# Scores and messages of an attention layer on a graph, made four tiles at a time: where the loop over the engines closes

## The chip, the cores and the metric

One Trainium2 chip, one core of it. The time is the device time of one execution in microseconds (us), median of three runs. The engines are TensorE (PE, with PEld for its weight loads), VectorE (DVE), ScalarE (ACT), GpSimd (POOL, which here issues the indirect transfers) and SyncE (SP, which issues the plain ones). Each has its own queue of instructions and takes them in order; engines wait for each other by semaphores that only count up.

## The reference

Two layers of attention on a graph of 6250 nodes and 100000 edges, sorted by target node, 8 heads of 16 features, 8 relations:

```python
k, q, v = (typed_linear(x, ntype, W).reshape(n, H, HS) for W in (Wk, Wq, Wv))
...
kw = rel_apply(k[src], etype, Watt)
a = (kw * q[dst]).sum(-1) * pri[:, etype].T / SQRT_D
amax = jax.ops.segment_max(a, dst, num_segments=n)
ex = jnp.exp(a - amax[dst])
den = jax.ops.segment_sum(ex, dst, num_segments=n)
alpha = ex / (den[dst] + 1e-16)
m = rel_apply(v[src], etype, Wmsg)
agg = jax.ops.segment_sum(alpha[..., None] * m, dst, num_segments=n)
```

Behind it come a typed linear, a gate, a layer norm, and after the second layer an output product.

## The kernel before

A node stage puts key and value of each node and relation, already multiplied by the relation's matrices, into a table in memory (`node_kv`, 256 numbers a row), and the queries into `node_q`. The edge stage (`edge_stage`, L1141) then goes over the edges once for each of the two layers. Edges are cut into 784 tiles of 128 (one edge a partition), 14 tiles are a batch (`G`), and there are 56 batches. Within a batch tiles are taken in fours (`FOURS`: 4, 4, 4 and 2 tiles).

Three batches are in flight. Step b of the stage works on batch b ("new"), b - 1 ("mid") and b - 2 ("old"), and each engine has its part of the step written out by hand in a function `step`, whose order is the order of its queue.

- POOL gathers the rows of the edges' sources from `node_kv`, one transfer a tile (L1243), into `rows`, which has three buffers. The tiles of four of batch b + 1 may be gathered as soon as TensorE has summed the same four of batch b - 2.
- SP loads for every tile the window of 128 queries that its targets lie in (`qw`, L1216) and the ranks of the edges in it.
- New: VectorE makes a one-hot matrix of the ranks (`one_hot`, L1259); TensorE spreads the queries to the edges with it (`spread`, L1499), and VectorE multiplies keys by them in place (`products`, L1270). A reduction over 16 features gives the scores (`scores`, L1275), `score[P, 14, 8]`. TensorE also turns the one-hot matrix (`turn`, L1488), and ScalarE copies it (L1424).
- Mid: TensorE transposes the scores of the batch (L1511), 8 x 14 rows. VectorE finds maxima over the runs of equal targets by scans (`own_maxima`, L1286 to L1292), ScalarE takes the exponential (L1439), VectorE sums and divides (`own_shares`, L1297 to L1305). TensorE transposes the result back (`alpha_ps`, L1526). `joined_tops` (L1310 to L1318) and `joined_sums` (L1323 to L1338) carry runs over tile borders; the latter's last instruction writes `share`. TensorE multiplies it out (`scale_ps`, L1539), ScalarE copies it (L1457). `messages` (L1355) multiplies the values by alpha in place.
- Old: TensorE sums the messages to target nodes (`sums`, L1480), VectorE multiplies the first column by the scale (`gains`, L1348), ScalarE adds all of it to `acc` (`means`, L1415 and L1419).

At the end of its step ScalarE makes the flags for the next maxima (`flags`, L1431 and L1432), and `own_maxima` waits for them and for the transposed scores. TensorE's step begins with two spreads of new and the transpose of mid's scores, and ends with the product for the scale.

Of the kernel before, what the change touches and what calls it, by code (L numbers as in the profile page):

```python
# [25 lines left out]
P = 128  # L26
N = 6250
E = 100000
D = 128
H = 8  # L30
HS = D // H
# [10 lines left out]
U = 3  # L42
# [1090 lines left out]
SIZES = (G,) * (B - 1) + (14,)  # L1133
BATCHES = len(SIZES)
FIRST = tuple(sum(SIZES[:b]) for b in range(BATCHES + 1))
FOURS = tuple(tuple(range(g, min(g + FOUR, n)) for g in range(0, n, FOUR)) for n in SIZES)
GROUP = tuple(sum(len(fours) for fours in FOURS[:b]) for b in range(BATCHES + 1))
# [3 lines left out]
def edge_stage(nc, c, s, rows_in, spent, l, tab, scratch, acc, weights):  # L1141
# [10 lines left out]
    with ExitStack() as st:  # L1152
# [8 lines left out]
        score = sb("score", [P, G, H])  # L1161
# [39 lines left out]
        with nc.Block(no_gpsimd_drain=True) as block:  # L1201
# [48 lines left out]
            def _(dve):  # L1250
# [18 lines left out]
                    dve.wait_ge(s["spread"], GROUP[b] + k + 1)  # L1269
                    v.tensor_tensor(half, half, ps_q[(GROUP[b] + k) % 2][:, 0:len(four), :], ALU.mult).then_inc(s["prod"], 1)  # L1270

                def scores(b):
                    n = SIZES[b]
                    dve.wait_ge(s["prod"], GROUP[b + 1])
                    v.reduce_sum(score[:, 0:n, :], rows[b % U][:, 0:n, 0:D].rearrange("p g (h d) -> p g h d", h=H),  # L1275
                                 axis=AX.X).then_inc(s["score"], 1)

                def of_tiles(a, rows_):
# [3 lines left out]
                def own_maxima(b):  # L1282
                    m = SIZES[b] * H
                    dve.wait_ge(s["score_t"], b + 1)
                    dve.wait_ge(s["flags"], 2 * b + 2)
                    v.tensor_tensor_scan(fwd[0:m, :], seam[0:m, 0:P], score_t[0:m, :], -BIG, ALU.add, ALU.max).then_inc(s["chain"], 1)  # L1286
                    dve.wait_ge(s["chain"], b * CHAIN + 1)
                    v.tensor_tensor_scan(top[0:m, ::-1], seam[0:m, 1:P + 1][:, ::-1], fwd[0:m, ::-1], -BIG, ALU.add, ALU.max).then_inc(s["chain"], 1)
                    dve.wait_ge(s["chain"], b * CHAIN + 2)
                    v.tensor_tensor(shifted[0:m, :], score_t[0:m, :], top[0:m, :], ALU.subtract).then_inc(s["shifted"], 1)  # L1290
                    mask, two = of_tiles(top, m)
                    v.tensor_tensor(ends[0:m, 0:2, :], mask, two, ALU.mult).then_inc(s["ends"], 1)  # L1292
# [55 lines left out]
                    v.tensor_tensor(gained[q % 2][:, 0:len(four)], ps_sum[q % 2][:, 0:len(four), 0], scale[b % 2][:, 1, four[0]:four[-1] + 1],  # L1348
                                    ALU.mult).then_inc(s["gained"], 1)

                def messages(b):
                    n = SIZES[b]
                    dve.wait_ge(s["alpha_ps"], b + 1)
                    half = rows[b % U][:, 0:n, D:2 * D].rearrange("p g (h d) -> p g h d", h=H)
                    v.tensor_tensor(half, half, alpha_ps[:, 0:n * H].rearrange("p (g h o) -> p g h o", h=H, o=1).to_broadcast([P, n, H, HS]),  # L1355
                                    ALU.mult).then_inc(s["message"], 1)

                def step(b):
                    new, mid, old = in_flight(b)
                    has = lambda batch, k: batch is not None and k < len(FOURS[batch])  # L1360
                    if has(new, 0):
                        products(new, 0)
                    if mid is not None:
                        own_maxima(mid)
                    if has(old, 0):
                        gains(old, 0)
                    if has(new, 1):
                        products(new, 1)
                    if b + 1 < BATCHES:
                        one_hot(b + 1)  # L1370
                    if mid is not None:
                        own_shares(mid)
                    if has(old, 1):
                        gains(old, 1)
                    if has(new, 2):
                        products(new, 2)
                    if mid is not None:
                        joined_tops(mid)
                    if has(new, 3):
                        products(new, 3)  # L1380
                    if has(old, 2):
                        gains(old, 2)
                    if mid is not None:
                        messages(mid)
                        joined_sums(mid)
                    if has(old, 3):
                        gains(old, 3)
                    if new is not None:
                        scores(new)

                v.memset(acc[:, :], 0.0).then_inc(s["zeroed"], 1)
                v.memset(tops[:, 0:1], -BIG).then_inc(s["zeroed"], 1)
# [76 lines left out]
            def _(pe):  # L1469
                t = nc.tensor  # L1470

                def sums(b, k):
                    q = GROUP[b] + k
                    if k == 0:
                        pe.wait_ge(s["message"], b + 1)
                        pe.wait_ge(s["turned"], GROUP[b + 1])
                    if q >= 2:
                        pe.wait_ge(s["joined"], UNTIL[q - 2])
                    for n, g in enumerate(FOURS[b][k]):
                        ins = t.matmul(ps_sum[q % 2][:, n, :], rows[b % U][:, g, D:2 * D], hot[b % U][:, g, :], start=True, stop=True)  # L1480
                    ins.then_inc(s["sums"], 1)
# [20 lines left out]
                def step(b):  # L1502
# [4 lines left out]
                            spread(new, k)  # L1507
                    if mid is not None:
                        m = SIZES[mid] * H
                        pe.wait_ge(s["score"], mid + 1)  # L1510
                        t.transpose(score_t[0:m, :], score[:, 0:SIZES[mid], :].rearrange("p g h -> p (g h)"), c["ident"][:, :]).then_inc(s["score_t"], 1)  # L1511
                    if has(old, 0):
                        sums(old, 0)
# [97 lines left out]
```

## Time and profile before

| what | value |
|---|---|
| median of three runs | 2824.23 us (2822.65 to 2825.16) |
| the profiled execution | 2824.39 us, of which the span from first to last instruction is 2822.7 us |
| PE busy | 1902.4 us (67%) |
| VectorE busy | 2146.3 us (76%) |
| ScalarE busy | 1519.7 us (54%) |
| POOL busy | 1971.6 us (70%) |
| granted TensorE clock, mean | 0.772 |

A row of the timeline gives the start, the duration, the engine, the line, the operation, what it writes and reads, and in brackets how long the engine stood idle before it and what it waited for. Busy shares are means over node stages and edge stages; neither edge stage's limit can be read from them.

### The profile page before, as it was taken

How to read it: one execution, taken by the hardware profiler on the slowest of the kernel's cores; microseconds unless marked ns; L12 is line 12 of the kernel's file. 1: busy time of each engine (PE TensorE's matmuls, PEld its weight loads, DVE VectorE, ACT ScalarE, POOL GpSimd, SP SyncE). 2: the span in 40 equal slices, each digit the busy share in tenths (PEclk: the TensorE clock that was granted, in tenths of full speed). 3: DMA queues.
4: the chain of work that ended last, by engine and by line, in shares of the span. 5: the costliest groups of instructions: out<-in, count | busy, mean ns of one | idle time of the engine just before them, and what ended most of it. 6: DMA issues, size and time to landing. Idle time of an engine off the chain costs nothing. (4 is left out here: it accounts for less than half of the span.)

```text
span 2822.7 us, 53679 instructions
## 1 busy us (share of the span) xinstructions
PE 1902.4 (67%) x12612; PEld 1692.1 (60%) x12612; DVE 2146.3 (76%) x5513; ACT 1519.7 (54%) x5159; POOL 1971.6 (70%) x2072
## 2 busy tenths in 40 slices
PE   1877747766777767776577747777777767667466
PEld 1755536666666666666455546666666666666344
DVE  6977758777777777777577757777777777777587
ACT  0027625555555555555577725555555555555555
POOL 3716667777777777777277777777777777777176
PEclk8569968777787787777688967778778787787655
DMA  5528876666666666665266776666666666665411
GB/s 135 88 109 346 342 204 186 185 184 183 186 184 184 185 184 185 185 185 169 68 244 276 292 203 184 184 184 183 184 185 183 183 184 184 183 184 163 116 45 37
DMA packets 396315, 512.23 MB, mean 181 GB/s; under 512 B 75449, under 2 KB 311419, under 8 KB 383508
## 3 DMA queue, kind: packets, MB, share of 16 engines
q0 software_dynamic: 102144, 327.28, 37.3%
q1 hardware_dynamic: 284760, 179.79, 21.8%
q10 hardware_dynamic: 9104, 1.86, 0.4%
q8 instruction: 97, 1.59, 0.2%
q14 instruction: 210, 1.72, 0.2%
HBM read 383.54 MB, written 142.96 MB: 187 GB/s over the span
## 5 line engine op out<-in xcount | busy, mean ns | idle before, releaser
L1243 POOL DMA_INDIRECT g_rows<-node_kv,g_ids x1568 | 1485.0, 947 | 474.8 <-issue 444.2
L1499 PE MATMUL g_ps_q<-g_qw,g_hot_t 128*128 128x128 f32 x3136 | 593.7, 357 | 61.8 <-DMA g_qw<-node_q 50.0
L1419 ACT ACTIVATE acc<-acc,g_gained,g_scale x1568 | 600.9, 383 | 3.0 <-issue 2.1
L1499 PEld LDWEIGHTS g_ps_q<-g_qw,g_hot_t 128*128 128x128 f32 x3136 | 546.6, 265 | 71.2 <-DMA g_qw<-node_q 51.6
L1415 ACT ACTIVATE acc<-g_ps_sum 128x127 f32 x1568 | 411.5, 262 | 317.5 <-DVE g_gained L1348 257.3
L1480 PE MATMUL g_ps_sum<-g_hot,g_rows 128*128 128x128 f32 x3136 | 553.6, 331 | 5.9 <-ACT acc L1419 5.7
L1480 PEld LDWEIGHTS g_ps_sum<-g_hot,g_rows 128*128 128x128 f32 x3136 | 512.0, 245 | 12.5 <-ACT acc L1419 8.4
L1270 DVE TENSOR_TENSOR g_rows<-g_rows,g_ps_q 128x512 f32<-128x512 f32 x448 | 274.5, 613 | 317.4 <-DMA g_rows<-node_kv,g_ids 290.0
L1488 PE MATMUL g_ps_hot<-ident,g_hot_t 128*128 128x128 f32 x1568 | 293.3, 312 | 18.2 <-ACT g_hot L1424 17.9
L1424 ACT ACTIVATE g_hot<-g_ps_hot 128x512 f32<-128x512 f32 x448 | 233.2, 521 | 56.1 <-PE g_ps_hot L1488 56.1
L1488 PEld LDWEIGHTS g_ps_hot<-ident,g_hot_t 128*128 128x128 f32 x1568 | 230.2, 169 | 28.0 <-ACT g_hot L1424 25.1
L1539 PE MATMUL g_ps_b<-g_share,head_of_feature 8*128 8x28 f32 x224 | 61.5, 359 | 264.2 <-DVE g_share L1338 259.3
L1525 PE MATMUL g_ps_a<-g_ends,head_of_row 112*8 112x56 f32 x224 | 30.6, 221 | 292.4 <-DVE g_alpha L1305 292.4
L1259 DVE TENSOR_TENSOR g_hot_t<-g_rank_row,g_ps_a 128x1792 f32<-128x1792 bf16 x112 | 225.5, 2014 | 0.1
L1539 PEld LDWEIGHTS g_ps_b<-g_share,head_of_feature 8*128 8x128 f32 x224 | 47.9, 264 | 295.6 <-DVE g_share L1338 290.2
L1275 DVE TENSOR_REDUCE g_score<-g_rows 128x112 f32<-128x1792 f32 x112 | 225.0, 2009 | 0.1
L1355 DVE TENSOR_TENSOR g_rows<-g_rows,g_ps_b 128x1792 f32<-128x1792 f32 x112 | 224.5, 2005 | 0.0
L1089 POOL DMA_INDIRECT n_ag<-node_agg,node_slot x112 | 116.9, 1044 | 137.5 <-DMA node_agg<-n_agg 46.4
L1439 ACT ACTIVATE g_exp_t<-g_shifted 112x128 f32<-112x128 f32 x112 | 34.7, 310 | 312.9 <-DVE g_shifted L1290 312.9
L1525 PEld LDWEIGHTS g_ps_a<-g_ends,head_of_row 112*8 112x8 f32 x224 | 13.5, 87 | 316.0 <-issue 316.0
L1052 PE MATMUL n_wide<-bd,n_kv_t 32*128 32x256 f32 x1792 | 140.9, 431 | 79.5 <-DVE n_kv L865 39.9
L865 DVE COPY n_kv<-n_wide 128x512 f32<-128x512 f32 x224 | 143.9, 684 | 49.3 <-PE n_wide L1052 36.3
(243 smaller groups left out, 3265.1 us busy)
## 6 DMA issues: line engine op xcount, KB each, us to landing
g_qw<-node_q SPq DMA_DIRECT2D x1568, 64.0 KB
g_rank_row<-edge_rank SPq DMA_DIRECT2D x112, 448.0 KB
g_rows<-node_kv,g_ids POOLq DMA_INDIRECT x1568
node_agg<-n_agg SPq DMA_DIRECT2D x24, 256.0 KB, 3.1
node_rows<-node_x SPq DMA_DIRECT2D x2, 1792.0 KB
node_q<-l_blank_q SPq DMA_DIRECT2D x1, 3200.0 KB
node_q<-n_q_sb,node_slot POOLq DMA_INDIRECT x112
node_kv<-n_kv,node_id POOLq DMA_INDIRECT x112
```

The lines of the kernel that those rows point to most:

```text
L865: v.tensor_copy(kv[i % KV][:, :, :, q * 32:(q + 1) * 32].rearrange("p r a f -> p a r f"), wide[:, q, :].rearrange("p (a r f) -> p a r f", ...
L1243: g_.indirect_dma_start(out=rows[b % U][:, g, :], out_offset=None, in_=scratch["kv"][:, :], in_offset=bass.IndirectOffsetOnAxis(ap=ids[b / ...
L1259: v.tensor_tensor(hot_t[b % 2][:, 0:n, :].rearrange("p g e -> p (g e)"), rank_row[:, 0:n * P], number_ps.to_broadcast([P, n * P]), ALU.is_ ...
L1270: v.tensor_tensor(half, half, ps_q[(GROUP[b] + k) % 2][:, 0:len(four), :], ALU.mult).then_inc(s["prod"], 1)
L1275: v.reduce_sum(score[:, 0:n, :], rows[b % U][:, 0:n, 0:D].rearrange("p g (h d) -> p g h d", h=H), axis=AX.X).then_inc(s["score"], 1)
L1355: v.tensor_tensor(half, half, alpha_ps[:, 0:n * H].rearrange("p (g h o) -> p g h o", h=H, o=1).to_broadcast([P, n, H, HS]), ALU.mult).then ...
L1415: a.activation(acc[:, bass.ds(w + 1, P - 1)], ps_sum[q % 2][:, n, 1:P], ACT.Copy).then_inc(s["copied"], 1)
L1419: a.activation(at, at, ACT.Identity, scale=scale[b % 2][:, 0, g:g + 1], bias=gained[q % 2][:, n:n + 1]).then_inc(s["joined"], 1)
L1424: a.activation(hot[b % U][:, four[0]:four[-1] + 1, :], ps_hot[q % 2][:, 0:len(four), :], ACT.Copy).then_inc(s["turned"], 1)
L1480: ins = t.matmul(ps_sum[q % 2][:, n, :], rows[b % U][:, g, D:2 * D], hot[b % U][:, g, :], start=True, stop=True)
L1488: ins = t.transpose(ps_hot[q % 2][:, n, :], hot_t[b % 2][:, g, :], c["ident"][:, :])
L1499: ins = t.matmul(ps_q[q % 2][:, n, :], hot_t[b % 2][:, g, :], qw[b % 2][:, g, :], start=True, stop=True)
```

## The change

VectorE's `scores` and `messages` get a second argument, the number of the four tiles, and do only these; `step` calls them piece by piece. The scores of the new batch stood at the end of the step; their pieces now stand behind `own_maxima`, behind `own_shares`, behind the third products and behind the third gains. The four pieces of the messages stand where the one instruction stood, behind the last of the scores. TensorE's waits for scores, messages and turned one-hot matrices count fours of tiles.

```diff
-                def scores(b):
-                    n = SIZES[b]
-                    dve.wait_ge(s["prod"], GROUP[b + 1])
-                    v.reduce_sum(score[:, 0:n, :], rows[b % U][:, 0:n, 0:D].rearrange("p g (h d) -> p g h d", h=H),
+                def scores(b, k):
+                    part_ = slice(FOURS[b][k][0], FOURS[b][k][-1] + 1)
+                    dve.wait_ge(s["prod"], GROUP[b] + k + 1)
+                    v.reduce_sum(score[:, part_, :], rows[b % U][:, part_, 0:D].rearrange("p g (h d) -> p g h d", h=H),
                                  axis=AX.X).then_inc(s["score"], 1)
...
-                def messages(b):
-                    n = SIZES[b]
-                    dve.wait_ge(s["alpha_ps"], b + 1)
-                    half = rows[b % U][:, 0:n, D:2 * D].rearrange("p g (h d) -> p g h d", h=H)
-                    v.tensor_tensor(half, half, alpha_ps[:, 0:n * H].rearrange("p (g h o) -> p g h o", h=H, o=1).to_broadcast([P, n, H, HS]),
+                def messages(b, k):
+                    first, n = FOURS[b][k][0], len(FOURS[b][k])
+                    if k == 0:
+                        dve.wait_ge(s["alpha_ps"], b + 1)
+                    half = rows[b % U][:, first:first + n, D:2 * D].rearrange("p g (h d) -> p g h d", h=H)
+                    v.tensor_tensor(half, half, alpha_ps[:, first * H:(first + n) * H].rearrange("p (g h o) -> p g h o", h=H, o=1).to_broadcast([P, n, H, HS]),
                                     ALU.mult).then_inc(s["message"], 1)
...
                     if mid is not None:
                         own_maxima(mid)
+                    if has(new, 0):
+                        scores(new, 0)
...
                     if mid is not None:
                         own_shares(mid)
+                    if has(new, 1):
+                        scores(new, 1)
...
                     if has(new, 2):
                         products(new, 2)
+                        scores(new, 2)
...
+                    if has(new, 3):
+                        scores(new, 3)
+                    for k in range(4):
+                        if has(mid, k):
+                            messages(mid, k)
                     if mid is not None:
-                        messages(mid)
                         joined_sums(mid)
                     if has(old, 3):
                         gains(old, 3)
-                    if new is not None:
-                        scores(new)
...
-                    if k == 0:
-                        pe.wait_ge(s["message"], b + 1)
-                        pe.wait_ge(s["turned"], GROUP[b + 1])
+                    pe.wait_ge(s["message"], q + 1)
+                    pe.wait_ge(s["turned"], q + 1)
...
-                        pe.wait_ge(s["score"], mid + 1)
+                        pe.wait_ge(s["score"], GROUP[mid + 1])
```

VectorE's queue from the last instruction of `joined_sums` to the first gains of the next step, before (`g_score` are the scores, `g_top` the maxima, `g_share` the share, `g_gained` the gains):

```order
L1338 TENSOR_TENSOR g_share<-g_part,g_whole 8x28
L1348 TENSOR_TENSOR g_gained<-g_ps_sum,g_scale 128x2
L1275 TENSOR_REDUCE g_score<-g_rows 128x112
L1270 TENSOR_TENSOR g_rows<-g_rows,g_ps_q 128x4x128
L1286 SCALAR_TENSOR_TENSOR g_ps_a<-g_seam,g_ps_a 112x128
L1288 SCALAR_TENSOR_TENSOR g_top<-g_seam,g_ps_a 112x128
L1290 TENSOR_TENSOR g_shifted<-g_ps_a,g_top 112x128
L1292 TENSOR_TENSOR g_ends<-tile_mask,g_top 112x28
L1348 TENSOR_TENSOR g_gained<-g_ps_sum,g_scale 128x4
```

The same place in the changed kernel:

```order
L1338 TENSOR_TENSOR g_share<-g_part,g_whole 8x28
L1348 TENSOR_TENSOR g_gained<-g_ps_sum,g_scale 128x2
L1270 TENSOR_TENSOR g_rows<-g_rows,g_ps_q 128x4x128
L1286 SCALAR_TENSOR_TENSOR g_ps_a<-g_seam,g_ps_a 112x128
L1288 SCALAR_TENSOR_TENSOR g_top<-g_seam,g_ps_a 112x128
L1290 TENSOR_TENSOR g_shifted<-g_ps_a,g_top 112x128
L1292 TENSOR_TENSOR g_ends<-tile_mask,g_top 112x28
L1275 TENSOR_REDUCE g_score<-g_rows 128x32
L1348 TENSOR_TENSOR g_gained<-g_ps_sum,g_scale 128x4
```

The reduction has gone from between the share and the next batch's first products, and a piece of it stands behind the maxima. The other pieces of the same step and those of the messages, further down the queue of the changed kernel (`g_alpha` is alpha; rows of small instructions between are left out by the dots):

```order
L1305 TENSOR_TENSOR g_alpha<-g_exp_t,g_ps_a 112x128
L1275 TENSOR_REDUCE g_score<-g_rows 128x32
L1348 TENSOR_TENSOR g_gained<-g_ps_sum,g_scale 128x4
L1270 TENSOR_TENSOR g_rows<-g_rows,g_ps_q 128x4x128
L1275 TENSOR_REDUCE g_score<-g_rows 128x32
...
L1270 TENSOR_TENSOR g_rows<-g_rows,g_ps_q 128x2x128
L1348 TENSOR_TENSOR g_gained<-g_ps_sum,g_scale 128x4
L1275 TENSOR_REDUCE g_score<-g_rows 128x16
L1356 TENSOR_TENSOR g_rows<-g_rows,g_ps_b 128x4x128 x3
L1356 TENSOR_TENSOR g_rows<-g_rows,g_ps_b 128x2x128
L1323 SCALAR_TENSOR_TENSOR g_coeff<-tile_pass_sb,g_grown 8x14
```

All of these pieces now stand between `own_maxima` and the share. TensorE's queue from the product for the scale on has the same instructions in the same order in both; of before, with the semaphores that each waits for:

```order
L1539 MATMUL g_ps_b<-g_share,head_of_feature 128x28 [waits edges_share]
L1499 MATMUL g_ps_q<-g_qw,g_hot_t 128x128 [waits edges_prod,edges_hot_t,edges_q_in1]
L1499 MATMUL g_ps_q<-g_qw,g_hot_t 128x128 x3
L1499 MATMUL g_ps_q<-g_qw,g_hot_t 128x128 [waits edges_prod]
L1499 MATMUL g_ps_q<-g_qw,g_hot_t 128x128 x3
L1511 MATMUL g_ps_a<-ident,g_score 112x128 [waits edges_score]
```

The transpose of the scores stays the last of these.

## Rows read from the trace of the kernel before

**Rows 1.** Waits of POOL, whole span, and a group of the page.
```profile
POOL g_rows L1243 <- PE g_ps_sum L1480: 23.8, 78, 0.3
...
L1243 POOL DMA_INDIRECT g_rows<-node_kv,g_ids x1568 | 1485.0, 947 | 474.8 <-issue 444.2
```

**Rows 2.** Timeline of VectorE, `own_maxima` of steps 1, 2 and 55, both layers.
```profile
397.12 0.42 DVE L1286 TENSOR_TENSOR_SCAN g_ps_a<-g_seam,g_ps_a 112x128 f32<-112x128 bf16 x1
...
413.25 0.43 DVE L1286 TENSOR_TENSOR_SCAN g_ps_a<-g_seam,g_ps_a 112x128 f32<-112x128 bf16 x1 [0.78 <-PE g_ps_a L1511]
...
1342.98 0.43 DVE L1286 TENSOR_TENSOR_SCAN g_ps_a<-g_seam,g_ps_a 112x128 f32<-112x128 bf16 x1 [0.87 <-PE g_ps_a L1511]
...
1658.46 0.42 DVE L1286 TENSOR_TENSOR_SCAN g_ps_a<-g_seam,g_ps_a 112x128 f32<-112x128 bf16 x1
...
1674.85 0.42 DVE L1286 TENSOR_TENSOR_SCAN g_ps_a<-g_seam,g_ps_a 112x128 f32<-112x128 bf16 x1
...
2605.44 0.43 DVE L1286 TENSOR_TENSOR_SCAN g_ps_a<-g_seam,g_ps_a 112x128 f32<-112x128 bf16 x1 [0.53 <-PE g_ps_a L1511]
```

**Rows 3.** Timeline of VectorE, one step of layer 1, to the next maxima.
```profile
1902.93 0.42 DVE L1286 TENSOR_TENSOR_SCAN g_ps_a<-g_seam,g_ps_a 112x128 f32<-112x128 bf16 x1
...
1904.57 0.16 DVE L1348 TENSOR_TENSOR g_gained<-g_ps_sum,g_scale 128x4 f32<-128x4 f32 x1 [0.34 <-issue]
...
1911.03 0.69 DVE L1270 TENSOR_TENSOR g_rows<-g_rows,g_ps_q 128x512 f32<-128x512 f32 x1 [1.49 <-DMA g_rows<-node_kv,g_ids]
1911.63 0.22 DVE L1310 TENSOR_TENSOR_SCAN g_tops<-tile_pass_sb,g_tops,g_ps_a 8x14 f32<-8x14 bf16 x1
...
1912.45 0.40 DVE L1270 TENSOR_TENSOR g_rows<-g_rows,g_ps_q 128x256 f32<-128x256 f32 x1
1912.78 0.14 DVE L1348 TENSOR_TENSOR g_gained<-g_ps_sum,g_scale 128x4 f32<-128x4 f32 x1
1912.85 2.00 DVE L1355 TENSOR_TENSOR g_rows<-g_rows,g_ps_b 128x1792 f32<-128x1792 f32 x1
1914.78 0.15 DVE L1323 SCALAR_TENSOR_TENSOR g_coeff<-tile_pass_sb,g_grown 8x14 f32<-8x14 bf16 x1
...
1916.16 0.18 DVE L1338 TENSOR_TENSOR g_share<-g_part,g_whole 8x28 f32<-8x28 f32 x1
...
1916.35 2.01 DVE L1275 TENSOR_REDUCE g_score<-g_rows 128x112 f32<-128x1792 f32 x1
...
1920.98 0.43 DVE L1286 TENSOR_TENSOR_SCAN g_ps_a<-g_seam,g_ps_a 112x128 f32<-112x128 bf16 x1 [0.39 <-PE g_ps_a L1511]
```

**Rows 4.** Timeline of TensorE, end of the same step and start of the next.
```profile
1913.31 0.44 PE L1488 MATMUL g_ps_hot<-ident,g_hot_t 128*128 128x128 f32 x2 [0.81 <-ACT g_hot L1424]
1916.40 0.62 PE L1539 MATMUL g_ps_b<-g_share,head_of_feature 8*128 8x28 f32 x2 [2.65 <-DVE g_share L1338]
1916.95 3.78 PE L1499 MATMUL g_ps_q<-g_qw,g_hot_t 128*128 128x128 f32 x16
1920.52 0.42 PE L1511 MATMUL g_ps_a<-ident,g_score 128*112 128x128 f32 x1
```

**Rows 5.** Windows: length, then busy time by engine, granted clock (PEclk), DMA share, GB/s.
```profile
1916.95:1920.94 3.99, 3.99 (x19) 3.99 (x19) 2.10 (x2) 2.01 (x8) 3.08 (x4) 0.50 0.75 213
...
619.20:621.80 2.60, 2.57 (x22) 2.53 (x23) 2.00 (x2) 1.76 (x8) 2.13 (x4) 1.00 0.78 200
```

**Rows 6.** Timeline of VectorE and TensorE, the same place of a step in layer 0.
```profile
619.00 0.18 DVE L1338 TENSOR_TENSOR g_share<-g_part,g_whole 8x28 f32<-8x28 f32 x1
...
619.23 0.40 PE L1539 MATMUL g_ps_b<-g_share,head_of_feature 8*128 8x28 f32 x2 [1.98 <-DVE g_share L1338]
...
621.45 0.27 PE L1511 MATMUL g_ps_a<-ident,g_score 128*112 128x128 f32 x1
```

**Rows 7.** Timeline: the flags in the step of rows 3; layer 0's tail.
```profile
1919.04 0.39 ACT L1432 ACTIVATE g_same<-seam_flags,ones 112x129 bf16<-112x129 bf16 x1
...
1358.88 0.43 DVE L1286 TENSOR_TENSOR_SCAN g_ps_a<-g_seam,g_ps_a 112x128 f32<-112x128 bf16 x1 [1.18 <-ACT g_same L1432]
```

## The prediction

> **What bounds the kernel now.** I read the waits of POOL first. Each of the 1568 gathers of edge rows keeps POOL busy 0.95 us, and the 444.2 us of idle time before them are its own issue, about 0.3 us each; the waits for TensorE's sums come to 23.8 us in 78 pieces of at most 0.3 us, which is that same issue time [rows 1]. So POOL never stands still for a buffer. In the edge stage a batch of 14 gathers sets the pace: `own_maxima` (L1286), whose start I call M, comes in step 2 of layer 0 at 413.25 and in step 55 at 1342.98, which is 17.54 us a step; in layer 1 it is (2605.44 - 1674.85) / 53 = 17.56 [rows 2]. I use 17.55.
>
> The next question is how near a second bound is. The steps are tied together by a **loop over three engines**, which I followed in the timeline of VectorE and of TensorE. From M, VectorE works down to `joined_sums`, whose last instruction (L1338) writes the share; call its end S. TensorE's queue then has the two scale matmuls (L1539), which wait for the share, the eight `spread` matmuls of the next batch (16 records), and only then the transpose of the scores (L1511), without which the next M cannot come.
>
> First half: M at 1902.93, S at 1916.16 + 0.18 = 1916.34, so 13.41 us [rows 3]. It holds two waits that are not work of the loop: 0.34 before the first gains and 1.49 before the third products, for a transfer. Without them, and with the 0.08 us of overlap that each of the two starts would have back, 13.41 - 0.34 - 1.49 - 0.16 = 11.42 us.
>
> Second half: the scale matmuls start 0.06 after S, the spreads at 1916.95, and the transpose ends at 1920.52 + 0.42 = 1920.94, 4.60 after S; M follows 0.04 later, and the row names this transpose as what it waited for [rows 3, 4]. It is that long since TensorE runs at 1.2 GHz (granted clock 0.50) [rows 5], after it stood idle 2.65 us for the share [rows 4]. The other form is at 2.4 GHz: after 1.98 us of idle time the transpose ends at 621.45 + 0.27 = 621.72, 2.54 after S at 619.18 [rows 5, 6]. I measured S to the end of the transpose in 106 steps: 83 lie between 4.0 and 4.6, mean 4.46, after idle times of 2.5 us in the mean; 16 lie under 3.5, nearly all after some 1.6 to 2 us.
>
> So the loop now needs 11.42 + 4.46 + 0.04 = 15.9 us of 17.55, and has **1.6 us to spare**. That is why POOL sets the pace. Note what stands in the second half on VectorE: the 2.01 us of `scores`, at 1916.35, just behind S. It fills time in which VectorE would wait for TensorE, and costs the loop nothing.
>
> **The change, part by part.**
> 1. Scores in four pieces, moved. One reduction of 1792 elements a row goes from behind S, and four come between M and S. A reduction and a multiply of 1792 elements take the same, 2.01 and 2.00, so I price pieces by the multiply: 512 elements last 0.69 and the next instruction starts 0.60 after it; 256 last 0.40, the next 0.33 after [rows 3]. Pieces 0 and 1 add 0.60 each. Piece 2 stands directly behind the products that it reads and waits for their end: 0.69 + 0.03 (a dependent pair has about 0.03 between) = 0.72. Piece 3, with a gain between, 0.35. Sum 2.27.
> 2. Messages in four pieces: 3 x 0.60 + 0.33 = 2.13, against 1914.78 - 1912.85 = 1.93 for one: 0.20.
> 3. First half of the loop: 11.42 + 2.27 + 0.20 = 13.89. Waits inside go: the third products now come to their turn 1.2 us later, so their transfer is mostly there.
> 4. Second half: the scores are ready long before, but TensorE takes the transpose in its turn, behind share, scale and spreads. Nothing of the 4.46 + 0.04 goes. The idle time before the scale matmuls grows: TensorE's last work before it ended at 1913.31 + 0.44 = 1913.75 [rows 4], 10.8 after M; 13.89 - 10.8 = 3.1 us idle instead of 2.65, so the slow form is the rule.
> 5. Loop: 13.89 + 4.50 = **18.39 us**, 0.84 over POOL's 17.55. The loop is now the pace. POOL's three batches of buffers don't help, since the loop is serial from the first batch to the last; POOL is only made to wait.
> 6. TensorE's finer waits (`message` and `turned` by four tiles): nothing. Behind them in its queue stand the turns and the next spreads, but both signals come a step earlier, so the sums still follow the transpose at once.
> 7. What the score pieces push back: the first gains by 0.6 us and the second by 1.2, and ScalarE's means with them. Covered: ScalarE's next meeting with the loop is the scale, behind S, and S itself is 2.5 later. The one-hot comes 0.6 later in its step and is used in the next. No DMA is added or moved on any queue.
>
> The skill has another figure for item 1. The Trainium skill, "VectorE: DVE Perf Modes", in the section on the TRN2 errata, gives a fixed 58 cycles (60 ns) for an instruction on SBUF data in its table, and says below it that 150 are measured. The trace sides with the second: (2.00 - 0.69) us over 1280 elements leaves 0.69 - 0.52 = 0.17 us fixed [rows 3]. By 60 ns the six extra instructions would cost 0.36 us of busy time and the loop would be some 0.3 us shorter, which would be an estimate of 2890 us.
>
> **Sum**, against the profiled execution's own time, 2824.4 us (span 2822.7 and 1.7 around it; the median of the three runs is 2824.23, so both agree to 0.01%):
> - 2 layers x 53 steps x 0.84 = 89;
> - the head: M of step 1 is bound by the first transfers and stays, at 397.12 and 1658.46. A step without gains is 0.2 shorter: 18.2 later are 415.3 and 1676.7, against 413.25 and 1674.85 [rows 2]: 2.1 + 1.8 = 4;
> - the tail of a layer: M to S is 12.7 in step 55 (1358.88 less 3.2 for the flags, as in A, less 1342.98 [rows 2, 7]) and grows to 13.9; step 56 has the 0.2 of the messages: 1.4 a layer, 3 in all. Behind S here ScalarE's flags decide (the wait of 1.18 at 1358.88 [rows 7]), as before.
>
> Together 96, so 2824.4 + 96 = **2921 us**, 3.4% slower.
>
> **Bounds of what the trace does not show.** Low: pieces with no fixed cost (1.93 + 0.13 for scores, nothing for messages) make the first half 13.48; with 4.13 + 0.04, the lower of the two lengths that the slow form mostly has, the loop is 17.65, and 106 x 0.10 + 5 gives 2840. High: 0.05 more for each of the eight pieces and always 4.64 make 14.29 + 4.64 = 18.93; 106 x 1.38 + 8 gives 2979. I take the middle since the 512-element row is the very shape.
>
> **Rivals.**
> A. *TensorE at full clock, and the loop stays hidden* (not slower). If the transpose ends 2.54 after S, ScalarE's path decides: the scale, two tiles' means and the flags end at 1919.04 + 0.39 = 1919.43, 3.09 after S [rows 7], and M 0.1 later. The loop is 13.89 + 3.19 = 17.08, under 17.55; only the tails stay: 2824.4 + 3 = 2827. The point of decision is 3.66 from S to M. For it: 16 steps of 106. Against: they came after short idle times, and the change lengthens them. Page's rule that would give this: the Trainium skill, "TensorE: Matmul & The Clock Gate", in Part 1, says that for modelling the cold ramp is under 1% of a typical kernel's span. By that rule the half clock would be left out and the time would be A's; here the trace disagrees, with 4.60 against 2.54 us in a loop that is run 112 times. Chance 0.11.
> B. *TensorE stays slow for more of the step.* Now it returns to full clock about 5 us after the scale matmuls. If the low clock held on until alpha is transposed, joined tops would wait and the loop would gain some 0.5 us: 18.9, 106 x 0.5 = 53 more, 2974. For it: less of each step busy. Against: the order of TensorE's work up to that point is unchanged. Chance 0.09.
> C. *Faster*: scores that are ready earlier save TensorE some waiting for them in the tail. But behind that the wait for the flags stands [rows 7], and POOL's gathers, 1.25 us each, are untouched; at most 3 us in all. With all that I may have overlooked, 0.03.
> The forecast has 0.76, and what is left, 0.01, is no change by other ways.
>
> **How the numbers follow.** What a measurement can tell from no change is 0.2%, 5.6 us. Slower: forecast and B, 0.85. Same: A and the rest, 0.12. Faster: 0.03. The range takes in most of the span between the bounds and B: 2850 to 2985; outside lie A, C and the outermost costs, about 0.2.
>
> **What would show it.** In the new profile: starts of `own_maxima` 18.4 us apart; POOL's gathers waiting for sums, some 90 us in all and up to a us or more at a time; VectorE's waits for gathered rows, like the 1.49 us of [rows 3], mostly gone, and in their place a wait of over a us before each `own_maxima` for the transpose; the idle time before the scale matmuls about 3.1 us, and TensorE at 0.50 behind it. It is wrong if the starts stay 17.55 apart: then the step to look at is S to M (item 4), or the price of the pieces (item 1).

## The result, and the profile after

| | before | after |
|---|---|---|
| median | 2824.69 us (4 runs, 2822.65 to 2826.42) | 2901.11 us (4 runs, 2897.57 to 2912.1) |
| span of the profiled execution | 2822.7 us | 2898.8 us |
| VectorE busy | 2146.3 us | 2193.7 us |
| POOL busy | 1971.6 us | 1972.3 us |
| granted TensorE clock, mean | 0.772 | 0.758 |

The changed kernel takes 1.0277 times as long, 95% interval 1.0249 to 1.0306: slower by 2.8%. The forecast was 2921 us, 3.4% slower.

First the pace. Timeline of VectorE in the changed kernel, `own_maxima` of steps 2 and 55 of both layers, which answers to [rows 2]:

```profile
410.83 0.43 DVE L1286 TENSOR_TENSOR_SCAN g_ps_a<-g_seam,g_ps_a 112x128 f32<-112x128 bf16 x1 [0.89 <-PE g_ps_a L1518]
...
1380.73 0.43 DVE L1286 TENSOR_TENSOR_SCAN g_ps_a<-g_seam,g_ps_a 112x128 f32<-112x128 bf16 x1 [0.64 <-ACT g_same L1440]
...
1713.62 0.43 DVE L1286 TENSOR_TENSOR_SCAN g_ps_a<-g_seam,g_ps_a 112x128 f32<-112x128 bf16 x1 [0.22 <-PE g_ps_a L1518]
...
2682.00 0.43 DVE L1286 TENSOR_TENSOR_SCAN g_ps_a<-g_seam,g_ps_a 112x128 f32<-112x128 bf16 x1 [1.16 <-PE g_ps_a L1518]
```

(1380.73 - 410.83) / 53 = 18.30 us a step in layer 0 and 18.27 in layer 1, against 17.54 and 17.56. POOL no longer sets it. Its waits over the whole span, which answer to [rows 1], each row with us in total, times and longest:

```profile
POOL g_rows L1243 <- issue: 438.6, 1427, 2.1
POOL g_rows L1243 <- PE g_ps_sum L1487: 100.8, 108, 2.5
```

The waits for TensorE's sums were 23.8 us in pieces of at most 0.3; now they are 100.8 us, up to 2.5 us at once. The gathers are as cheap as before, but are held up. On VectorE the transfer has almost gone out of the waits. Whole span, before and then after:

```profile
DVE g_rows L1270 <- DMA g_rows<-node_kv,g_ids: 290.0, 181, 6.8
```

```profile
DVE g_rows L1270 <- PE g_ps_q L1506: 275.3, 111, 14.8
DVE g_ps_a L1286 <- PE g_ps_a L1518: 110.7, 102, 1.2
...
DVE g_rows L1270 <- DMA g_rows<-node_kv,g_ids: 14.8, 3, 7.5
```

What VectorE waits for at a step's start is now TensorE, once for the spread queries and once more for the transposed scores, in nearly each of the 112 steps. One such start in the timeline of the changed kernel, with the slow form of TensorE's stretch (answers to [rows 4]):

```profile
1927.38 0.18 DVE L1338 TENSOR_TENSOR g_share<-g_part,g_whole 8x28 f32<-8x28 f32 x1
...
1927.61 0.62 PE L1546 MATMUL g_ps_b<-g_share,head_of_feature 8*128 8x28 f32 x2 [3.22 <-DVE g_share L1338]
1928.16 3.78 PE L1506 MATMUL g_ps_q<-g_qw,g_hot_t 128*128 128x128 f32 x16
...
1930.34 0.69 DVE L1270 TENSOR_TENSOR g_rows<-g_rows,g_ps_q 128x512 f32<-128x512 f32 x1 [2.70 <-PE g_ps_q L1506]
1931.73 0.42 PE L1518 MATMUL g_ps_a<-ident,g_score 128*112 128x128 f32 x1
...
1932.19 0.43 DVE L1286 TENSOR_TENSOR_SCAN g_ps_a<-g_seam,g_ps_a 112x128 f32<-112x128 bf16 x1 [1.16 <-PE g_ps_a L1518]
```

S, the end of the share, is 1927.56; from there to M at 1932.19 are 4.63 us, as before. Of these VectorE waits 2.70 and 1.16. Before, the reduction of the scores lay in that time.

### The profile page after: what moved, and what is told of

Its sections match the earlier page's. It is cut to its first block and busy times, and to the rows that moved or that the text cites. A ratio compares the mean times of both kernels' runs of the same rounds, so it can differ in the third digit from the quotient of the medians.

```text
span 2898.8 us, 54687 instructions
## 1 busy us (share of the span) xinstructions
PE 1923.1 (66%) x12612; PEld 1721.1 (59%) x12612; DVE 2193.7 (76%) x6185; ACT 1523.5 (53%) x5159; POOL 1972.3 (68%) x2072
## 5 line engine op out<-in xcount | busy, mean ns | idle before, releaser
L1506 PE MATMUL g_ps_q<-g_qw,g_hot_t 128*128 128x128 f32 x3136 | 601.9, 360 | 56.6 <-DMA g_qw<-node_q 49.3
L1506 PEld LDWEIGHTS g_ps_q<-g_qw,g_hot_t 128*128 128x128 f32 x3136 | 553.5, 267 | 63.9 <-DMA g_qw<-node_q 50.8
L1487 PE MATMUL g_ps_sum<-g_hot,g_rows 128*128 128x128 f32 x3136 | 574.7, 340 | 11.8 <-ACT acc L1427 11.8
L1487 PEld LDWEIGHTS g_ps_sum<-g_hot,g_rows 128*128 128x128 f32 x3136 | 539.4, 256 | 19.3 <-issue 18.8
L1270 DVE TENSOR_TENSOR g_rows<-g_rows,g_ps_q 128x512 f32<-128x512 f32 x448 | 273.2, 610 | 290.2 <-PE g_ps_q L1506 275.3
L1275 DVE TENSOR_REDUCE g_score<-g_rows 128x32 f32<-128x512 f32 x448 | 274.8, 613 | 4.1
L1356 DVE TENSOR_TENSOR g_rows<-g_rows,g_ps_b 128x512 f32<-128x512 f32 x448 | 246.5, 611 | 0.0
```

Of the source, the lines that this page charges most:

```text
L1275: v.reduce_sum(score[:, part_, :], rows[b % U][:, part_, 0:D].rearrange("p g (h d) -> p g h d", h=H), axis=AX.X).then_inc(s["score"], 1)
L1356: v.tensor_tensor(half, half, alpha_ps[:, first * H:(first + n) * H].rearrange("p (g h o) -> p g h o", h=H, o=1).to_broadcast([P, n, H, HS ...
L1506: ins = t.matmul(ps_q[q % 2][:, n, :], hot_t[b % 2][:, g, :], qw[b % 2][:, g, :], start=True, stop=True)
```

## The experiments

The loop theory: M to S on VectorE, and S to the next M through TensorE, add up to a step as soon as they are over POOL's 17.55 us. It has two rivals: the six extra instructions cost their time wherever they stand, or VectorE is simply too full. In the table below, M to S and S to M are means over steps 4 to 55 of both layers of the profiled execution; a step is the mean from step 2 to 55.

| kernel | M to S | S to M | step, layers 0 and 1 | median | ratio to before, 95% interval |
|---|---|---|---|---|---|
| before | 13.02 | 4.51 | 17.54, 17.56 | 2824.7 | 1 |
| changed | 14.04 | 4.20 | 18.30, 18.27 | 2901.1 | 1.0277 (1.0249 to 1.0306) |
| all score pieces behind the share | 13.17 | 4.42 | 17.61, 17.58 | 2827.3 | 0.9997 (0.9988 to 1.0007) |
| scale behind the transpose | 14.34 | 3.20 | 17.56, 17.56 | 2830.9 | 1.0013 (1.0004 to 1.0023) |
| TensorE kept busy | 14.38 | 3.22 | 17.58, 17.60 | 2829.8 | 1.0005 (0.9995 to 1.0015) |
| 0.6 us more in the loop | 14.71 | 4.08 | 18.89, 18.79 | 2962.5 | 1.0470 (1.0452 to 1.0487) |

The four lower kernels ran in one session, beside runs of the kernel before with a median of 2828.25 us. Where POOL sets the pace, the halves hold waits for transfers and add up to its pace.

**1. The same pieces, back at the old place.** If the number of instructions is what costs, this stays slow.

```diff
-                    if has(new, 0):
-                        scores(new, 0)
...
-                    if has(new, 1):
-                        scores(new, 1)
...
-                        scores(new, 2)
...
-                    if has(new, 3):
-                        scores(new, 3)
...
                     if has(old, 3):
                         gains(old, 3)
+                    if has(new, 0):
+                        scores(new, 0)
+                    if has(new, 1):
+                        scores(new, 1)
+                    if has(new, 2):
+                        scores(new, 2)
+                    if has(new, 3):
+                        scores(new, 3)
```

> The changed kernel with all four score pieces put back behind the share (end of VectorE's step); scores and messages stay in four pieces, TensorE's finer waits stay. Loop theory: M to S falls from 14.0 to 11.8 us, the pieces lie in the time in which VectorE waits for the transpose, the loop needs some 16 us and POOL's 17.55 us a step is the pace again: 2824 to 2828 us. Rival (the six extra instructions a step cost it, wherever they stand: 112 steps x 0.46 to 0.92 us of VectorE time): 2875 to 2895 us.

Measured 2827.33 us, 0.9997 of before. This kernel has all the cuts of the change, four score pieces and four message pieces, and TensorE's finer waits. The cutting alone costs nothing that can be told, as long as the score pieces lie behind the share. VectorE's waits for transfers are back, 156 of them where the kernel before had 181:

```profile
DVE g_rows L1270 <- DMA g_rows<-node_kv,g_ids: 224.3, 156, 6.7
```

**2. The other half shortened: TensorE's order.** VectorE's queue stays as changed. The scale's product leaves the head of the line.

```diff
                         pe.wait_ge(s["score"], GROUP[mid + 1])
+                        if old is not None:
+                            pe.wait_ge(s["chain"], old * CHAIN + 12)
                         t.transpose(score_t[0:m, :], score[:, 0:SIZES[mid], :].rearrange("p g h -> p (g h)"), c["ident"][:, :]).then_inc(s["score_t"], 1)
+                    if old is not None:
+                        pe.wait_ge(s["share"], old + 1)
+                        t.matmul(scale_ps[:, 0:2 * SIZES[old]], c["head_of_feature"][:, :], share[:, :, 0:SIZES[old]], start=True, stop=True).then_inc(s["scale_ps"], 1)
...
-                    if mid is not None:
-                        pe.wait_ge(s["share"], mid + 1)
-                        t.matmul(scale_ps[:, 0:2 * SIZES[mid]], c["head_of_feature"][:, :], share[:, :, 0:SIZES[mid]], start=True, stop=True).then_inc(s["scale_ps"], 1)
```

> The changed kernel, VectorE untouched; on TensorE the scale matmuls move from the end of a step to behind the transpose of the scores in the next step, and the transpose waits for the last read of the shared PSUM bank by joined_sums, some 1.1 us before S, in place of the share. Loop theory: spreads and transpose run before S, the second half becomes ScalarE's path, 3.1 to 3.2 us; loop 14.0 + 3.15 = 17.2 us, under POOL's 17.55: 2824 to 2832 us. Rival (VectorE is simply too full, 14 us and more in a row): no or little change, 2890 to 2905 us.

Measured 2830.93 us, 1.0013 of before: of the 76 us, 2.7 are left against the kernel before of the same session, with no instruction of VectorE moved or taken away. So VectorE is not too full. A step's start in its timeline (`own_maxima` is L1286, the scale L1523 here):

```profile
1017.70 0.16 DVE L1327 TENSOR_TENSOR g_add<-g_add,g_ps_a 8x14 f32<-8x14 f32 x1
1018.00 0.29 PE L1520 MATMUL g_ps_a<-ident,g_score 128*112 128x128 f32 x1 [0.38 <-DVE g_add L1327]
1018.84 0.18 DVE L1338 TENSOR_TENSOR g_share<-g_part,g_whole 8x28 f32<-8x28 f32 x1
...
1019.07 0.40 PE L1523 MATMUL g_ps_b<-g_share,head_of_feature 8*128 8x28 f32 x2 [0.78 <-DVE g_share L1338]
```

In this step the transpose ends 0.7 us before S (0.4 in the mean); in the changed kernel it ends 4.1 us behind S in the mean. S to M is now 3.2 us, which is the way through ScalarE's flags. The transpose goes no earlier in this kernel, since it writes into the tile `ps_a`, from which VectorE still reads the ends of the sums, and I made TensorE wait for the last of these reads.

**3. TensorE's clock.** The same order as in the changed kernel, but eight matmuls without use fill the idle time before the scale; they write where the next spread writes.

```diff
+                    if mid is not None and new is not None:
+                        if b + 1 < BATCHES:
+                            pe.wait_ge(s["prod"], GROUP[b + 1] - 1)
+                        for _ in range(8 if b + 1 < BATCHES else 0):
+                            t.matmul(ps_q[GROUP[b + 1] % 2][:, 0, :], c["ident"][:, :], c["ident"][:, :], start=True, stop=True)
```

> The changed kernel plus eight matmuls without use on TensorE (identity by identity into the bank that the next spread overwrites) in its idle time before the scale matmuls. If the half clock behind the idle time makes the second half long: share to transpose falls from 4.14 us (mean) to about 2.55, ScalarE's 3.15 us decide, loop 17.2 us, 2824 to 2835 us. If the clock has nothing to do with it: no gain, or slower by up to 1 us a step where the extra matmuls hold up the share's product, 2900 to 3000 us.

Measured 2829.82 us, 1.0005 of before. S to the end of the transpose is 2.56 us in the mean (2.54 to 3.50), from 4.14. The rows of one step:

```profile
1000.62 1.95 PE L1548 MATMUL g_ps_q<-ident 128*128 128x128 f32 x16
1002.74 0.17 DVE L1338 TENSOR_TENSOR g_share<-g_part,g_whole 8x28 f32<-8x28 f32 x1
...
1002.97 0.40 PE L1551 MATMUL g_ps_b<-g_share,head_of_feature 8*128 8x28 f32 x2 [0.40 <-DVE g_share L1338]
1003.30 2.05 PE L1506 MATMUL g_ps_q<-g_qw,g_hot_t 128*128 128x128 f32 x16
...
1005.18 0.27 PE L1518 MATMUL g_ps_a<-ident,g_score 128*112 128x128 f32 x1
```

The 16 spread records take 2.05 us here and 3.78 in the row at 1928.16 above. More work on TensorE made the kernel 71 us faster than the changed one, since TensorE comes out of the wait at 2.4 GHz: S to the end of the transpose is nowhere over 3.50 us now, where it was in 97 of 108 steps of the changed kernel (mean granted clock 0.813, from 0.758).

**4. The dose.** One reduction without use, 512 elements a row, in the loop; its result goes to a tile that nobody reads.

```diff
                     if has(new, 0):
                         scores(new, 0)
+                        v.reduce_sum(idle_[:, :], c["ones"][:, :].rearrange("p (o e) -> p o e", o=1).to_broadcast([P, FOUR, P]), axis=AX.X)
```

> The changed kernel plus one reduction without use (512 elements a row, about 0.61 us start to start) on VectorE behind the first score piece, between M and S. Loop theory: every step is 0.61 us longer, 106 x 0.61 = 65 and 1 for the tails: 2965 us. If VectorE had slack between M and S: about 2901 us.

Measured 2962.54 us, 1.0470 of before; the span is 2962.6 - 2898.8 = 63.8 us over the changed kernel's, where 65 for the steps and 1 for the tails were expected. A step grew by 0.59 us in layer 0 and 0.52 in layer 1, and POOL's waits for the sums with it:

```profile
POOL g_rows L1244 <- PE g_ps_sum L1489: 167.1, 136, 2.8
```

**5. Four kernels in sessions that answer less.** These ran twice, on two different chips, and there the kernel before itself took 3470.4 and 3459.4 us instead of 2828 (and 6360.3 us in one of its 13 runs in the first session).

The extra reduction behind the share (the end of VectorE's step) instead of in the loop:

```diff
                     if has(old, 3):
                         gains(old, 3)
+                    if new is not None:
+                        v.reduce_sum(idle_[:, :], c["ones"][:, :].rearrange("p (o e) -> p o e", o=1).to_broadcast([P, FOUR, P]), axis=AX.X)
```

> The changed kernel plus the same reduction without use (about 0.61 us), but behind the share, at the end of VectorE's step. Loop theory: it lies in the wait for the transpose and costs nothing: 2898 to 2905 us. If VectorE's busy time as such is the bound: 2965 us.

> The changed kernel plus the reduction without use (0.61 us) behind the share, run again since the kernel before took 3470 us in the session of the first try. Loop theory: it lies in the wait for the transpose and costs nothing: 2898 to 2905 us. If VectorE's busy time as such is the bound: 2965 us, as with the same instruction between M and S.

The messages in one instruction (`messages` is that of the kernel before again), the scores as changed:

```diff
-                    for k in range(4):
-                        if has(mid, k):
-                            messages(mid, k)
                     if mid is not None:
+                        messages(mid)
                         joined_sums(mid)
...
-                    pe.wait_ge(s["message"], q + 1)
+                    pe.wait_ge(s["message"], b + 1)
```

> The changed kernel with the messages in one instruction again, scores still in pieces between M and S. Loop theory: M to S is 0.20 us shorter, 107 x 0.20 = 21 less: 2880 us. Rival (pieces of the messages let TensorE start its sums earlier): 2901 us or slower.

> The changed kernel with the messages in one instruction, again for the same reason. Loop theory: M to S 0.20 us shorter, 21 us less: 2880 us. Rival (pieces of the messages let TensorE start its sums earlier): 2901 us or slower.

The kernel before with its one score instruction ahead of the messages:

```diff
+                    if new is not None:
+                        scores(new)
                     if mid is not None:
                         messages(mid)
...
-                    if new is not None:
-                        scores(new)
```

> The kernel before with its one score instruction moved ahead of the messages; nothing is cut in pieces. Loop theory: M to S is 11.42 + 1.98 = 13.4 us, the second half 4.2 (its mean in the changed kernel) to 4.5 us, loop 17.6 to 17.9 us: just over POOL's pace, 2830 to 2862 us. Rival (the cutting alone does the harm): 2824 us.

> The kernel before with its one score instruction moved ahead of the messages, again for the same reason. Loop theory: M to S 13.4 us, loop 17.6 to 17.9 us, 2830 to 2862 us. Rival (the cutting alone does the harm): 2824 us.

The last two score pieces behind the share, the first two as changed:

```diff
                         products(new, 2)
-                        scores(new, 2)
...
-                    if has(new, 3):
-                        scores(new, 3)
...
                         gains(old, 3)
+                    if has(new, 2):
+                        scores(new, 2)
+                    if has(new, 3):
+                        scores(new, 3)
```

> The changed kernel with the last two score pieces (768 of 1792 elements) behind the share and the first two where the change put them. Loop theory: M to S 14.04 - 1.07 = 12.97 us, loop 17.2 to 17.5 us, just under POOL's pace: 2825 to 2832 us. Rival (harm in proportion to the pieces that are moved): about 2860 us.

> The changed kernel with the last two score pieces behind the share, again for the same reason. Loop theory: M to S 12.97 us, loop 17.2 to 17.5 us, just under POOL's pace: 2825 to 2832 us. Rival (harm in proportion to what is moved): about 2860 us.

| kernel | first session | second session |
|---|---|---|
| before | 3470.4 | 3459.4 |
| half of the pieces behind the share | 3473.3, 0.9976 (0.9932 to 1.0020) | 3471.1, 1.0045 (1.0005 to 1.0084) |
| messages whole | 3513.6, 1.0119 (1.0051 to 1.0187) | 3509.3, 1.0143 (1.0067 to 1.0218) |
| changed, extra reduction behind the share | 3529.2, 1.0182 (1.0127 to 1.0237) | 3531.3, 1.0214 (1.0139 to 1.0290) |
| whole scores moved | 3669.4, 1.0591 (1.0533 to 1.0649) | 3662.0, 1.0570 (1.0483 to 1.0657) |

No expected time can be held against these. Where the time goes can be seen in part. In the traces of these kernels some instructions begin late although their engine is idle and the work they wait for has ended. One such place in the kernel with the reduction behind the share (second session), and then the same place in the changed kernel (`products` is L1271 and L1270; "remote" is a releaser that the profile can't name):

```profile
1017.78 1.09 PE L1509 MATMUL g_ps_q<-g_qw,g_hot_t 128*128 128x128 f32 x4
...
1019.74 0.15 DVE L1319 TENSOR_TENSOR g_below<-g_before,g_joint 8x14 f32<-8x14 f32 x1
1022.07 0.42 DVE L1271 TENSOR_TENSOR g_rows<-g_rows,g_ps_q 128x256 f32<-128x256 f32 x1 [2.17 <-remote]
```

```profile
1957.77 1.09 PE L1506 MATMUL g_ps_q<-g_qw,g_hot_t 128*128 128x128 f32 x4
...
1959.74 0.15 DVE L1318 TENSOR_TENSOR g_below<-g_before,g_joint 8x14 f32<-8x14 f32 x1
1959.82 0.40 DVE L1270 TENSOR_TENSOR g_rows<-g_rows,g_ps_q 128x256 f32<-128x256 f32 x1
```

The fourth products wait, by the program, for the spreads alone, which ended at 1018.87. In this kernel they begin over 1 us late in 43 of 102 steps and `joined_tops`, which waits for TensorE's product of the ends, in 52; in the changed kernel neither does once. Together these two come to 2.7 us a step, nearly all of what M to S has grown by (17.0 us from 14.04). Why, the profile doesn't show: whether the signal or the instruction itself came late is open. With such late starts a step takes over 21 us even with half of the pieces behind the share.

Only what these kernels say of each other in one session is left, and that is little. Half of the pieces behind the share costs 0.5% at most in the mean, as the loop theory has it; harm in proportion, the 2860 us of the expectation, would be some 1.2%. Moving the one whole instruction ahead of the messages, with nothing cut, is the dearest, 5.7 to 5.9%, where no theory expected more than 1.3%. Its third gains begin over 1 us late in 70 of 102 steps (up to 4.9 us, second session), so that the scores and messages behind them, 4 us of work, all come late; with the fourth products that is 4.1 us a step. So its size can't be read as the price of the place, and the place without the cutting stays untested in an undisturbed session. That the cutting alone does no harm is shown by experiment 1. That the reduction behind the share is free, and that whole messages give 21 us back, stays open: the changed kernel had no run in these sessions. The two kernels differ by 16 and 22 us, which would fit both. If VectorE's busy time were the bound, they should differ by 64 us or more; how far that holds in a disturbed session isn't known.

## Why the prediction was right

**What bounds before, and the loop (right).** Every reading of [rows 1 to 6] that carried the sum held: POOL was the pace, the loop the second bound with room to spare, and the room was filled by the moved pieces. Experiments 2 and 3 shorten the second half of the loop in two different ways, by TensorE's order and by its clock (the mean granted clock of the kernel rises in both, to 0.803 and 0.813), and both return to 17.6 us a step; experiment 4 lengthens the first half and is paid nearly in full.

**Items 1 to 3, the first half (right, 0.15 short).** Forecast 13.89 us, measured 14.04, median 13.97. The pieces last what the multiply's row said: 613 ns in the mean for the score pieces and 611 for the message pieces, each over three of 512 elements and one of 256, against 613 ns for the products before. From the third products to S, 5.31 + 0.72 + 0.35 + 0.20 = 6.58 was forecast, and 6.58 is the least measured (5.31 was the least before); the mean is 6.78. What a cut costs there is not the fixed term of a duration: an independent instruction starts some 0.08 us before the end of the one before it, and by item 2 a cut costs 0.20 / 3 = 0.07 us.

The fixed term itself is best read from the score reductions, which read SBUF alone (products and messages read PSUM too): 2009 ns over 1792 elements before, 680 over 512 in the pieces (ahead of the second bar a row gives the busy time in us and the mean of one in ns):

```profile
L1275 DVE TENSOR_REDUCE g_score<-g_rows 128x112 f32<-128x1792 f32 x112 | 225.0, 2009 | 0.1
```

```profile
L1275 DVE TENSOR_REDUCE g_score<-g_rows 128x32 f32<-128x512 f32 x336 | 228.4, 680 | 3.9
```

At the pace of the 1280 elements between, 512 take 532 ns, and some 150 ns are left. That agrees with the 150 cycles (some 155 ns) that the Trainium skill, "VectorE: DVE Perf Modes", section on the TRN2 errata, calls measured, and not with the 58 (60 ns) of its table. The prediction's estimate of 2890 us by the table has a step that isn't worked out, "some 0.3 us shorter": items 1 and 2 price the six extra instructions at 2.27 + 0.20 - 1.93 = 0.54 us. At the 0.36 us that the prediction takes from the table a step would be 0.18 us shorter, which makes an estimate of 2902 us. That 2890 or 2902 lies nearer to the measured time than 2921 does is chance, since the pieces cost what the rows said and the difference lies in the second half, the head and the tail.

**Where the other 0.2 us of some steps come from (a part of rival B).** TensorE has a second idle time in a step, before alpha. In steps 4 to 54 of both layers, 102 in all, the eight records of the sums behind it (L1487) take 1.06 us, which is the full clock, in 13 steps, 1.91 or 1.92, the half clock, in 51, and something between in 38. Before it was 38, 35 and 29. M to S is 13.87 us in the mean in the 13 and 14.19 in the 51. The changed kernel, step 15 of layer 1:

```profile
1957.26 0.34 PE L1532 MATMUL g_ps_a<-g_ends,head_of_row 112*8 112x56 f32 x2 [3.38 <-DVE g_alpha L1305]
...
1958.65 1.91 PE L1487 MATMUL g_ps_sum<-g_hot,g_rows 128*128 128x128 f32 x8
...
1960.66 0.16 DVE L1348 TENSOR_TENSOR g_gained<-g_ps_sum,g_scale 128x4 f32<-128x4 f32 x1 [0.44 <-issue]
...
1964.58 0.18 DVE L1338 TENSOR_TENSOR g_share<-g_part,g_whole 8x28 f32<-8x28 f32 x1
...
1964.81 0.40 PE L1546 MATMUL g_ps_b<-g_share,head_of_feature 8*128 8x28 f32 x2 [2.11 <-DVE g_share L1338]
1965.14 2.05 PE L1506 MATMUL g_ps_q<-g_qw,g_hot_t 128*128 128x128 f32 x16
```

And the clock over the two stretches (the number before the DMA share):

```profile
1957.26:1959.20 1.94, 1.94 (x10) 1.76 (x11) 1.91 (x5) 1.30 (x6) 1.33 (x3) 0.50 0.60 211
1965.14:1967.30 2.16, 2.16 (x20) 2.16 (x20) 0.69 (x1) 1.69 (x8) 1.75 (x2) 1.00 0.77 214
```

After 3.38 us of idle time the sums run at half clock, the third gains come 0.44 late, and the share with them. But then the clock is full when the share comes, and the spreads take 2.05 us. What this step loses in its first half, it gains more than back in the second. So it goes in 11 of the 51 steps, the only ones of the 102 in which S to the end of the transpose stays under 3.5 us; in the other 40 the second half is of the slow form as well.

**Item 4, the second half (right that nothing of it goes, 0.3 too long).** Forecast 4.50, measured 4.20. I put the mean of the slow form, 4.46 us to the end of the transpose, into every step, since the longer idle time would make that form the rule. It didn't: of 108 stretches 77 were of the slow form (4.0 us and more, mean 4.43), where the kernel before had 85, though the idle time before the scale grew from 2.36 to 2.71 us. Over all 108 the mean is 4.15 us; it was 4.18 before already, and with that figure the forecast would have been 0.28 us a step lower. The idle time is not the 3.1 us of the forecast either: TensorE's last work of the step was itself later in the steps where it ran at half clock.

**Item 5 (right).** 13.89 + 4.50 = 18.39 was forecast, 18.30 and 18.27 were measured. The two errors, 0.15 short and 0.30 long, cancel in part, and to that extent it is luck that the step came out within 0.12 us.

**The sum.** In spans, 2898.8 - 2822.7 = 76.1 us:
- the loop: 53 x (18.30 - 17.54) + 53 x (18.27 - 17.56) = 78, forecast 89;
- the head: step 1 to 2 takes 18.1 and 18.35 us, 18.2 forecast. In layer 0 the first `own_maxima` came at 392.74 instead of 397.12, 4.4 us earlier. That comes from ahead of the edge stage: POOL's first gather starts at 358.55 instead of 363.00, and the first `own_maxima` 34.2 us behind it, against 34.1. Nothing there was changed, and of the four kernels of experiments 1 to 4 three begin at 357.6 to 358.7 and one at 361.9, so it differs from execution to execution. The net of layer 0's head is -2.4 us where +2.1 was forecast:

```profile
363.00 1.01 POOL L1243 DMA_INDIRECT g_rows<-node_kv,g_ids  x1 [0.48 <-POOL g_ids L1232]
```

```profile
358.55 1.01 POOL L1243 DMA_INDIRECT g_rows<-node_kv,g_ids  x1 [0.48 <-POOL g_ids L1232]
```

- **the tail: this term failed, in size and sign.** I took 13.9 us for M to S in step 55. That step makes no one-hot, there being no next batch, and has 1.93 us less work. Before, the wait for the last transfers hid that (12.7 us); now the rows are there, and M to S is 1392.66 - 1380.73 = 11.93. The flags decide behind it, as forecast, which the wait of 2.88 shows:

```profile
1392.49 0.17 DVE L1338 TENSOR_TENSOR g_share<-g_part,g_whole 8x28 f32<-8x28 f32 x1
1392.60 0.16 DVE L1348 TENSOR_TENSOR g_gained<-g_ps_sum,g_scale 128x2 f32<-128x2 f32 x1
1395.64 0.43 DVE L1286 TENSOR_TENSOR_SCAN g_ps_a<-g_seam,g_ps_a 112x128 f32<-112x128 bf16 x1 [2.88 <-ACT g_same L1440]
```

From M of step 55 to M of step 56 are 14.91 us instead of 15.90, so a layer's tail is 1.0 shorter where I had it 1.2 longer. With the head of layer 1 and what follows the edge stages this makes 0.5 us. 89 + 4 + 3 was forecast, 78 - 2.4 + 0.5 came.

**Rival A (did not happen, and is real).** Experiment 3 is rival A made on purpose: at full clock the step is POOL's again and the time 2829.8 us, 2827 forecast for it. The Trainium skill, "TensorE: Matmul & The Clock Gate", Part 1, speaks of the warm-up when it puts the ramp, for modelling, at under 1% of a typical kernel's span. Taken for the whole cost of the half clock, as rival A takes it, it would have left out 71 us here, 2.5%, and the trace disagrees: the half clock comes back in most of the steps.

**Items 6 and 7 (item 6 right).** With the finer waits and all pieces at the old place the time is that of before (experiment 1). No experiment takes item 7, the later gains and one-hot, by itself.

No version beat the kernel before, nor could one of these: under 17.55 us a step POOL's 14 gathers of 1.25 us are the pace, and none of the edits touches them.

## What to carry to other kernels

An instruction of an engine that is idle elsewhere in the step is not free to move: ask which half of the loop between the engines it stands in, and add the halves up against the engine that sets the pace. Work that lies behind a signal which another engine takes 4 us to answer is hidden; the same work ahead of that signal is paid in every step. And the answering half can be shortened by the other queue's order, or by keeping TensorE busy while it waits, with nothing changed on the engine that looks full.

## What the runs showed that I had not expected

- TensorE's half clock moves about within the step. Of its two idle times, before alpha and before the share, it comes back slow from the one, from the other or from both, so the mean over all steps (4.14 us for S to the end of the transpose, between 2.54 and 4.61), and not that of the commonest form, is what to price with.
- Twice the kernel before ran over 22% longer in a whole session. In the kernels of these sessions VectorE begins work up to 5 us late that nothing in the profile holds back. Beside it the order of the kernels changed its sizes: the moved whole instruction cost 5.7 to 5.9% there, against 0.2 to 1.3% expected from the undisturbed rows.
